# Loading a filter as soon as its last two products are issued, in a float32 convolution by blocks

## What is computed

```
k_ = v_ = ctx (16 batches, 64 heads, 8 channels, 1024)     q_ = layernorm(x)
kv  = k_[i] * v_[j]                       for all pairs (i, j) of a head's 8 channels
y   = causal convolution of kv with ssm_kernel[head], 1024 taps   (+ kv * D)
out = sum over i of y[i, j] * q_[i]
x1  = x + tanh(g_xattn) * out
result = x1 + tanh(g_ffn) * experts(layernorm(x1))
```

## Time and profile before

| | us |
|---|---|
| median of 3 timed runs | 4374.21 (4369.9 to 4388.32) |
| profiled execution, its own time | 4357.41 |
| its span, first to last instruction | 4355.6 |
| TensorE busy in the span | 4130.0 |
| VectorE busy in the span | 2608.2 |
| ScalarE busy in the span | 1898.5 |

### The profile page before, as it was taken

One profiled execution on the slowest core, in us unless ns is written; L12 is line 12 of the kernel. 1 busy time (PEld: TensorE's weight loads), 2 busy tenths in 40 slices (PEclk: granted clock), 3 DMA queues, 4 the chain that ended last, 5 costly groups with the idle time before them and its releaser, 6 DMA issues.

```text
span 4355.6 us, 71272 instructions
## 1 busy us (share of the span) xinstructions
PE 4130.0 (95%) x25930; PEld 3766.7 (86%) x25930; DVE 2608.2 (60%) x2980; ACT 1898.5 (44%) x2451; POOL 997.7 (23%) x1200
## 2 busy tenths in 40 slices
PE   6999999999999999996899999999999999999997
PEld 6899999999999999996688888888888988988986
DVE  6899999999999999996434441222323332333331
ACT  6777777777777777774211111111112211121120
POOL 1232322232322332331000014451001211211111
PEclk9999999999999999998899999999999999999999
DMA  7878888878888888886532333423433443344332
GB/s 167 207 192 217 204 220 198 214 196 218 198 217 196 217 197 213 198 218 160 72 116 72 102 89 106 116 83 93 120 108 97 92 102 97 82 111 97 78 96 49
DMA packets 280375, 634.14 MB, mean 146 GB/s; under 512 B 45840, under 2 KB 111866, under 8 KB 280246
## 3 DMA queue, kind: packets, MB, share of 16 engines
q1 hardware_dynamic: 218582, 413.89, 31.6%
q0 software_dynamic: 61664, 218.41, 26.7%
HBM read 311.03 MB, written 170.16 MB: 110 GB/s over the span
## 4 chain that ended last, share of the span: by engine, by line
PE 48%; DMA 2%; DVE 1%; issue 1%; ACT 0%; SPq 0%; POOL 0%; DVEq 0%; POOLq 0%; ACTq 0%
PE moe_ps L1644 11%; PE moe_ps L1645 11%; PE moe_ps L1646 11%; PE moe_ps L1662 5%; PE moe_ps L1663 5%; PE moe_ps L1664 5%; PE moe_psT L1633 1%; DMA out<-moe_y,moe_add_i 1%; DVE moe_zl L1542 1%; DMA moe_y<-out 0%; ACT moe_zh L1314 0%; DMA out<-moe_y 0%; DVE moe_hid L1555 0%; DVE moe_y L1569 0%; DMA moe_zin<-zT_d 0%
## 5 line engine op out<-in xcount | busy, mean ns | idle before, releaser
L1644 PE MATMUL moe_ps<-moe_zh,moe_w1h 128*128 128x512 f32 (+2 forms) x2368 | 861.7, 364 | 36.9 <-DVE moe_zl L1542 22.9
L1645 PE MATMUL moe_ps<-moe_zl,moe_w1h 128*128 128x512 f32 (+2 forms) x2368 | 859.3, 363 | 0.0
L1646 PE MATMUL moe_ps<-moe_zh,moe_w1l 128*128 128x512 f32 (+2 forms) x2368 | 857.4, 362 | 0.0
L690 PE MATMUL att_psY<-att_kv_hi,att_tz_hi 128*128 128x288 f32 x2560 | 767.3, 300 | 40.2 <-DMA att_kv_lo<-att_kv 39.9
L692 PE MATMUL att_psY<-att_kv_hi,att_tz_lo 128*128 128x288 f32 x2560 | 756.0, 295 | 0.0
L691 PE MATMUL att_psY<-att_kv_lo,att_tz_hi 128*128 128x288 f32 x2560 | 755.6, 295 | 0.0
L1555 DVE TENSOR_TENSOR moe_hid<-moe_ps,moe_act_s 128x512 f32<-128x512 f32 (+2 forms) x148 | 91.6, 619 | 893.5 <-PE moe_ps L1646 869.5
L1644 PEld LDWEIGHTS moe_ps<-moe_zh,moe_w1h 128*128 128x128 f32 x2368 | 446.6, 189 | 89.8 <-issue 38.3
L690 PEld LDWEIGHTS att_psY<-att_kv_hi,att_tz_hi 128*128 128x128 f32 x2560 | 482.6, 189 | 41.2 <-issue 40.5
L1646 PEld LDWEIGHTS moe_ps<-moe_zh,moe_w1l 128*128 128x128 f32 x2368 | 447.9, 189 | 51.5
L1645 PEld LDWEIGHTS moe_ps<-moe_zl,moe_w1h 128*128 128x128 f32 x2368 | 447.2, 189 | 51.1 <-issue 0.2
(11 more groups left out here) (188 smaller groups left out, 7911.6 us busy)
## 6 DMA issues: line engine op xcount, KB each, us to landing
att_kv_lo<-att_kv POOLq DMA_DIRECT2D x128, 1152.0 KB, 13.4
att_kT<-in_cT SPq DMA_DIRECT2D x64, 512.0 KB, 12.8
att_xn<-in_x SPq DMA_DIRECT2D x64, 512.0 KB, 5.8
out<-att_x SPq DMA_DIRECT2D x64, 512.0 KB, 4.8
z_d<-att_z SPq DMA_DIRECT2D x64, 512.0 KB, 8.4
zT_d<-att_zT SPq DMA_DIRECT2D x64, 512.0 KB, 15.1
moe_zin<-zT_d SPq DMA_DIRECT2D x64, 512.0 KB, 5.0
moe_y<-out SPq DMA_DIRECT2D x128, 256.0 KB, 4.0
```

The lines of the kernel that those rows point to most:

```text
L690: nc.tensor.matmul(acc, w_hi[:, cols], x_hi, start=start, stop=False, skip_group_check=True)
L1644: nc.tensor.matmul(acc, w1h[:, c, cols], zh[:, c, 0:w], start=(c == 0), stop=False)
L1645: nc.tensor.matmul(acc, w1h[:, c, cols], zl[:, c, 0:w], start=False, stop=False)
L1646: last = nc.tensor.matmul(acc, w1l[:, c, cols], zh[:, c, 0:w], start=False, stop=(c == C - 1))
```

## The change

The load of S for head h + 1 is issued in step h, once y_7's two products with S are done for both halves of the batch. A new semaphore `sz_used` says so. On SP's list it stands behind `load_x` and ahead of `store_z`; for the first head it is issued at the start. For this, y_7 is done in two passes: S for both halves, then T for both halves. In y_4 and y_5, the products with S stand last, and y_4 waits for S right in front of each product with it and no longer at its beginning.

```diff
-        far = [("S", a + 2 - c, c) for c in (2, 3)] if a < 6 else [("S", a - c, c) for c in (0, 1)]
-        return far + [("T", a - c, c) for c in range(G, a + 1)]
+        near = [("T", a - c, c) for c in range(G, a + 1)]
+        if a < G + 2:
+            return near + [("S", a + 2 - c, c) for c in (2, 3)]
+        return [("S", a - c, c) for c in (0, 1)] + near
...
             def load_sums(h):
-                wait(sp, y_done, NT * h)
+                wait(sp, sz_used, h)
...
             load_keys(1)
+            load_sums(0)
 
             def step(h, u, ahead, back, back2):
-                load_sums(h)
                 if ahead:
                     load_filter(h + 1, 1 - u)
...
                 if ahead:
                     load_x(h + 1, 1 - u)
+                    load_sums(h + 1)
                 if back:
                     store_z(h - 1)
...
-                    pe.wait_ge(sz_in, 32 * h + 32)
...
-                for half in range(2):
-                    acc = psY[n % 2][:, half, 0:NB * PAIRS]
-                    if a >= G:
-                        pe.wait_ge(v_set, 4 * h + (2 if a % 2 else 0) + half + 1)
-                    for k, (kind, d, c) in enumerate(terms):
...
+                parts = [terms[:2], terms[2:]] if n == NT - 1 else [terms]
+                for part in parts:
+                    for half in range(2):
+                        acc = psY[n % 2][:, half, 0:NB * PAIRS]
+                        if a >= G and part is parts[0]:
+                            pe.wait_ge(v_set, 4 * h + (2 if a % 2 else 0) + half + 1)
+                        for term in part:
+                            kind, d, c = term
+                            if n == G and kind == "S":
+                                pe.wait_ge(sz_in, 32 * h + 32)
...
+                        if half == 0 and between is not None:
+                            between()
+                    if n == NT - 1 and part is parts[0]:
+                        last.then_inc(sz_used, 1)
                 last.then_inc(y_done, 1)
```

More of the change, by code:

```diff
@@ L202, in gated_conv @@
         tz_in = [m.sem(f"tz_in{u}") for u in range(2)]
-        sz_in = m.sem("sz_in")
+        sz_in, sz_used = m.sem("sz_in"), m.sem("sz_used")
         x1_out, z_out, zT_out, l_out = m.sem("x1_out"), m.sem("z_out"), m.sem("zT_out"), m.sem("l_out")
@@ L710, in conv @@
                 terms = blocks(a)
-                for half in range(2):
-                    acc = psY[n % 2][:, half, 0:NB * PAIRS]
-                    if a >= G:
-                        pe.wait_ge(v_set, 4 * h + (2 if a % 2 else 0) + half + 1)
-                    for k, (kind, d, c) in enumerate(terms):
[L716 to L720, removed]
+                parts = [terms[:2], terms[2:]] if n == NT - 1 else [terms]
[8 more added lines that the diff above has]
+                                pe.wait_ge(sz_in, 32 * h + 32)
+                            w_hi, w_lo, first = (tz_hi[u], tz_lo[u], 0) if kind == "T" else (sz_hi, sz_lo, 3)
+                            last = thrice(acc, w_hi, w_lo, d - first, half_of(kv_hi[u], NT - 1 - c, half),
+                                          half_of(kv_lo[u], NT - 1 - c, half), a < G and term is terms[0],
+                                          term is terms[-1])
+                        if half == 0 and between is not None:
+                            between()
+                    if n == NT - 1 and part is parts[0]:
+                        last.then_inc(sz_used, 1)
                 last.then_inc(y_done, 1)
```

## The result

The changed kernel takes 4343.47 us (median of 6 runs) against 4368.2 us for the kernel before (6 runs). The ratio is 0.9937, with a 95% interval of 0.9915 to 0.9960: 25 us faster, where 78 were forecast. The profiled execution took 4343.53 us around a span of 4341.7 us, 13.9 us less than the span before.

A forecast was written before the change was run, and what follows sets the result against it. TensorE's stall for sz_lo was taken to bound each head, with VectorE close behind. TensorE's side came to about 85 us, VectorE's to 84 - 6 = 78, the gain taken: 4374.2 to 4296 us, range 4278 to 4338.

The forecast's parts named there:

- The sums' stall: TensorE's wait for sz_lo in front of y_4, 92.1 us or 1.49 us a head, was to go.
- the load leaves about 3 us earlier: On SP's queue the sums' load was to move to about 999.13, 3.2 us earlier.
- the two passes of y_7 and the repeated waits: On TensorE, the split of y_7 and y_4's repeated waits on sz_in: taken as 0, upper bound 33 us.
- `minus_v`'s wait: TensorE's 5.4 us wait for minus_v was to shrink to near nothing, with the keys out about 2.5 us earlier.
- the next late transfer: The second half of kv_lo, needed at y_4, was to be late next on TensorE, 0.45 us a head.
- VectorE's own round: VectorE's own work and short pauses in the convolution, 29.76 us a head, were to become the bound.
- no more than 84.0: Most that VectorE's side could gain over 62 heads: its waits of 77.8 us for TensorE and 6.2 for ScalarE.
- about 0.2 us a head on TensorE's side: Gain (+12 us) from transfers leaving earlier and meeting kv_lo with shorter packets, bringing TensorE's side to about 85 us.
- the wait that I had put at 28 us: TensorE's wait at y_4 for kv_lo's second half: 0.45 us a head, 28 us in all, with its flight unchanged.
- rival A: kv_lo takes the sums' place at y_4: flight 13.8 us, gain 39 us, about 4331 us; chance 0.20.
- the 84 - 6: VectorE as the bound: 84 us of waits less 0.1 us a head for hand-overs, a gain of 78 us.
- the flight of 11.8 us: One kv_lo flight with z's store issued earlier, 11.8 us not 13.6, read as earlier traffic not lengthening it.

The follow-up runs named there:

- e1: Changed kernel, with SP issuing keys and filter only once kv_lo's second half has landed; 4261.4 us, ratio 0.9781.
- e12: Kernel before, with keys, filter and z's store issued only once kv_lo's second half has landed, nothing of the change; 4264.5 us, ratio 0.9789.
- e2: Kernel before with TensorE's new order alone, the sums still loaded at the head's start; 4350.7 us, ratio 0.9980.
- e9: Changed kernel, loading only the high half of the filter after the first two heads; 4287.3 us, ratio 0.9843.
- e10: Changed kernel without the loads of the sums after the first head; 4309.4 us, ratio 0.9892.
- e11: Changed kernel with z's store moved later on SP's list, behind the load of x, filter still issued at once; 4262.6 us, ratio 0.9782.
- e4: As e1, with z's store too moved behind the landing of kv_lo's second half; 4257.5 us, ratio 0.9775.
- e5: Changed kernel with SP's loads of keys and filter swapped, keys first, both still issued at once; 4269.2 us, ratio 0.9795.
- e8: Changed kernel without the filter's loads after the first two heads, keys still issued at once; 4258.8 us in one run.
- e7: As e4, without two of VectorE's four multiplications per half; 4221.4 us, ratio 0.9689.
- e3: Changed kernel with the sums' products first in y_4 and y_5, as before; 4343.5 us, ratio 0.9961.
- e6: Kernel before, with only keys and filter issued once kv_lo's second half has landed; 4270.6 us, ratio 0.9794.

## Why the prediction was wrong

**Right.** The sums' stall goes whole (92.1 to 0), the load leaves about 3 us earlier, and the two passes of y_7 and the repeated waits cost nothing that shows: TensorE's round, from y_4's first product to the last `shared` product before the next y_4, has a median of 29.05 us before and 29.00 after. `minus_v`'s wait shrinks from 5.4 to 1.5 us. `kv_lo` was named as the next late transfer, VectorE's own round as the next bound. That floor was measured: in e1, where it binds, the line that answers to the earlier trace rows is

```profile
L572 DVE TENSOR_TENSOR att_diff<-att_kv x63: 1333/1344/1373, 61.6 to 1902.9; 128x1152 f32<-128x1152 f32 x63
```

and (1902.9 - 61.6) / 62 = 29.70 us a head, against 29.76 worked out. The bound of "no more than 84.0" on VectorE's side was a little low with it: e1's 62 heads take 88.2 us less than those of the kernel before, e12's 90.6.

**Wrong.** The step that failed is the one in the sum: "The transfers leave earlier and meet `kv_lo` with shorter packets, which I value at about 0.2 us a head on TensorE's side (+12, so about 85)". Its sign was wrong. The flight of `kv_lo` went from 13.04 to 14.11 us, 1.07 us longer, and with it the wait that I had put at 28 us "if its flight stays as it is" came out at 72.9. The condition was what failed: in e2, where the flight stays (13.06 us), y_4 starts 0.39 us a head late for `kv_lo`, near the 0.45 taken. The longer flight is what rival A described, with its flight of 13.8 us too short by 0.3 and its time of 4331 too low by 12; it had 0.20 of the chances. With `kv_lo` this late, VectorE did not become the bound, and the 84 - 6 built on it did not come into play.

**How it comes about.** Before, the sums took the 2.5 us of SP's queue between z and the filter. Moved ahead, they land 2.0 and 3.2 us after the issue of `kv_lo`, whose own first data packet starts at 2.1 us. But all that stood behind them moves up: the filter is issued 1.7 us after `kv_lo` instead of 4.3, the keys 4.5 us instead of 8.7 (means of the 58 flights). So more of it falls into `kv_lo`'s flight, 1.87 MB instead of 1.25, and of the filter 0.66 MB instead of 0.13. I had weighed the moved transfer against its new neighbours, and not the queue that closes up behind it. Taking away any one piece of that traffic shortens the flight and gives time back: half the filter (e9), the sums (e10), z (e11), the filter and keys (e1), all three late (e4). Keys ahead of the filter do it too, with the amount unchanged (e5). That the cause is the traffic of SP's queue beside `kv_lo` is shown by these, and that the filter straight behind z's store is the costly part of what moved up. Why the filter's transfers and z's store cost more than as many megabytes of keys stays open.

The row that misled me was the flight of 11.8 us with z's store a little earlier. It was the shortest of the 58 flights of the kernel before, which run from 11.8 to 13.6 us, and so no measure of what earlier traffic does.

**The sum with measured terms.** TensorE's waits went from 98 to 80.4 us, 18 less. Against it stand the stretches at half speed: seven in the changed kernel's convolution instead of five, each some 1.7 us, 3 us more. That leaves some 14 to 15, where the spans differ by 13.9. The medians differ by 25; the profiled execution before was 11 us below its median, and the one after at it. For the differences between other kernels the same two terms come short by some us (e9 against the changed kernel: 36 us of waits and 12 of half speed, in 55). A part lies outside the convolution: from the last L567 (or its like) to the end the profiled executions take 2354 us (e1, e4) to 2365 us (before, changed), and e12, whose convolution is e4's, 2364. Why that stage differs stays open.

**The last completion packet.** The Trainium skill, "DMA: Bandwidth & Descriptors", section "Queues, rings and completion order", has the completion's write land after all earlier writes of the engine, across queues. In the mean of the 58 flights the last data packet of `kv_lo` starts at 11.38 us and the last completion packet at 12.72 in the kernel before, at 12.13 and 13.80 in the changed one, and at 10.61 and 10.96 in e1, where the queue is empty by then. That agrees with it: the gap is 1.3 and 1.7 us with traffic behind, 0.35 without. It doesn't give the size: in e8, with the most traffic but for e9 and no filter, the gap is 0.5 us (12.05 and 12.55). I took the rule for one about the sums and z, in front. Without the sums (e10) the gap is no smaller, 1.95 us, so what is issued after `kv_lo` counts too.

## What to carry to other kernels

Moving a transfer ahead on a queue moves everything behind it too. Before valuing such a move, list what will then run beside the transfer that is late next, and hold non-urgent loads and stores back until that one has landed: here this alone, in the kernel before, gave 2.1% (e12), more than three times the change. A stall in front of one operation with two late operands is worth only the difference between the two, and no more than the slack of the next engine.

## What the runs showed of the hardware

- A flight of 1.18 MB took 8.5 us (e7) to 15.3 us (e3) with the same packets of its own, by what the other queue had on at the time.
- The other queue's megabytes don't order the flights: 1.35 MB beside one of 13.81 us (e10), 1.97 MB beside one of 12.89 us (e8). A store of 0.5 MB out of the flight made it 2.3 to 2.4 us shorter in three pairs (changed and e11, e1 and e4, e6 and e12).
- The kernel before had five stretches of 3.41 us at a granted clock of 0.5 in the convolution stage, the changed one seven (two of them below; the column before DMA's is the granted clock). Each of the twelve begins within 1.5 us of the end of a stall of TensorE of 1.7 to 2.4 us; most stalls of that size, and the longest, 3.0 us, have none behind them. In e1, e4 and e12, where no wait of TensorE is above 1.3 us, the stage has none at all from 61 us to its end. It has none in e2, e6, e9 and e10 either, where the longest stall is 1.6 to 1.9 us.

```profile
572.20:575.60 3.40, 3.40 (x17) 3.40 (x16) 3.37 (x4) 0.00 (x0) 0.00 (x0) 0.50 1.08 271
...
1596.20:1599.60 3.40, 3.40 (x18) 3.40 (x17) 3.27 (x5) 0.65 (x1) 0.00 (x0) 0.50 1.05 251
```
